# A fused decoder block on one core: the last three passes in an order of their own, and the mixing stage over a ring of seven single-stream PSUM banks

## What is computed

```python
x = x + attention(layernorm(x))          # 32 heads, 8 key/value heads, rope, causal
x = x + autocorrelation(layernorm(x), ctx, ctx)   # 8 heads; FFT correlation, top 9 lags, softmax, shifted sum
x = x + ffn(layernorm(x))
```

```python
H_res  = sinkhorn_log(x_norm @ W_res.T + base)    # 4x4, 50 iterations: rows, then columns normalised
H_pre, H_post = softmax(...), softmax(...)        # 4 each
H_res  = (1 - g) * I + g * H_res
y      = (sum_n x_streams[n] * H_pre[n]) @ W_branch
out[i] = sum_j H_res[i, j] * x_streams[j] + y * H_post[i]
```

## Time and profile before

| | |
|---|---|
| runs | 1224.99 us median of 3 (1220.55 to 1226.48) |
| profiled execution, its own time | 1223.23 us |
| its span, first to last instruction | 1221.4 us |
| mean granted TensorE clock | 0.931 of full speed |
| PE, DVE, ACT, POOL busy | 84%, 75%, 49%, 36% of the span |

### The profile page before, as it was taken

One profiled execution on the slowest core, in us unless ns is written; L12 is line 12 of the kernel. 1 busy time (PEld: TensorE's weight loads), 2 busy tenths in 40 slices (PEclk: granted clock), 3 DMA queues, 4 the chain that ended last, 5 costly groups with the idle time before them and its releaser, 6 DMA issues. The chain is left out here.

```text
span 1221.4 us, 23230 instructions
## 1 busy us (share of the span) xinstructions
PE 1028.0 (84%) x7866; PEld 759.1 (62%) x7866; DVE 921.5 (75%) x2819; ACT 596.9 (49%) x1789; POOL 442.5 (36%) x619
## 2 busy tenths in 40 slices
PE   5889999999999999999657999999999897615056
PEld 4667777777777787777445677776555554313034
DVE  6756787666787666786614878778999999996994
ACT  6534545544555544455515667766564564212023
POOL 0613443333443333443313766663433343110020
PEclk9989999999999999999778999999999998857579
DMA  9011011111011111011132222422222211148025
GB/s 380 29 59 42 17 58 58 58 58 41 22 53 58 58 58 41 29 48 42 45 102 86 87 91 74 130 91 74 89 92 97 77 54 39 44 135 326 0 52 138
DMA packets 47234, 95.71 MB, mean 78 GB/s; under 512 B 5952, under 2 KB 30400, under 8 KB 47168
## 3 DMA queue, kind: packets, MB, share of 16 engines
q1 hardware_dynamic: 47168, 94.91, 23.1%
HBM read 64.48 MB, written 27.26 MB: 75 GB/s over the span
## 5 line engine op out<-in xcount | busy, mean ns | idle before, releaser
L628 POOL TENSOR_TENSOR prob_G<-prob_G,rl 128x512 f32<-128x512 f32 x96 | 99.8, 1041 | 250.4 <-DVE rl L513 250.4
L390 ACT ACTIVATE prob_G<-prob_G,negm 128x128 f32<-128x128 f32 x384 | 148.8, 388 | 83.9 <-DVE negm L455 83.9
L245 PE MATMUL ps_qkv<-w_hi,xT_hi 128*128 128x512 f32 x384 | 156.3, 407 | 17.4 <-DVE prob_G L518 9.2
L246 PE MATMUL ps_qkv<-w_lo,xT_hi 128*128 128x512 f32 x384 | 151.0, 393 | 0.0
L247 PE MATMUL ps_qkv<-w_hi,xT_lo 128*128 128x512 f32 x384 | 150.8, 393 | 0.0
L319 PE MATMUL ps_qkv<-wo_hi,aT_hi 128*128 128x512 f32 x256 | 108.5, 424 | 0.0
L321 PE MATMUL ps_qkv<-wo_hi,aT_lo 128*128 128x512 f32 x256 | 102.6, 401 | 0.0
L320 PE MATMUL ps_qkv<-wo_lo,aT_hi 128*128 128x512 f32 x256 | 102.4, 400 | 0.0
L245 PEld LDWEIGHTS ps_qkv<-w_hi,xT_hi 128*128 128x128 f32 x384 | 72.7, 189 | 44.6 <-issue 21.8
L451 DVE TENSOR_TENSOR prob_G<-ps_s,mask 128x512 f32<-128x512 f32 x96 | 64.9, 676 | 44.4 <-PE ps_s L228 43.9
L480 DVE TENSOR_TENSOR xT_lo<-ps_t,xT_hi 128x512 fp32r<-128x512 f32 x16 | 11.1, 692 | 100.2 <-ACT xT_hi L418 100.2
(11 more groups left out here) (252 smaller groups left out, 2658.2 us busy)
## 6 DMA issues: line engine op xcount, KB each, us to landing
xin<-in_x SPq DMA_DIRECT2D x16, 512.0 KB, 3.3
xres<-in_x SPq DMA_DIRECT2D x16, 512.0 KB, 5.5
x<-xres SPq DMA_DIRECT2D x16, 512.0 KB, 2.6
c_xin<-x SPq DMA_DIRECT2D x16, 512.0 KB, 4.3
c_b_xres<-x SPq DMA_DIRECT2D x16, 512.0 KB, 3.2
rows_x<-c_row SPq DMA_DIRECT2D x64, 128.0 KB, 2.3
m_xm<-rows_x SPq DMA_DIRECT2D x16, 512.0 KB, 8.7
out<-m_ot SPq DMA_DIRECT2D x64, 128.0 KB, 2.4
```

Source lines behind the costliest of these rows:

```text
L245: nc.tensor.matmul(ps_qkv[:, n, :], xT_hi[:, k, :], w_hi[:, k, cols], start=k == 0, stop=False)
L246: nc.tensor.matmul(ps_qkv[:, n, :], xT_hi[:, k, :], w_lo[:, k, cols], start=False, stop=False)
L390: r = nc.scalar.activation(prob(g)[:, j, :], prob(g)[:, j, :], ACT.Exp, bias=negm[:, h:h + 1], accum_out=lsum[:, h:h + 1])
L628: nc.gpsimd.tensor_tensor(prob(g), prob(g), rl[:, g * GROUP:(g + 1) * GROUP].rearrange("p (j o) -> p j o", o=1).to_broadcast([P, GROUP, T] ...
```

## The change

- Chain a gets steps earlier: 10 instead of 6 by the end of pass 6, and 40 instead of 2 in pass 7; its halfway logarithms fall in pass 10 instead of 11. Chain b gets 14 steps instead of 6 in pass 14, chain a 15 instead of 40.
- In pass 14 the weights of row 15 are scaled on DVE, in eight instructions of 128x128, instead of one of 128x1024 on POOL (L1436).
- Passes 15 to 17 are replaced by a function `ending` on PE, ACT and DVE. The products of row 15 are done in halves of 512 columns; no logarithm stands before the copies of the transposed weights on ACT; the DVE takes 2 steps of each of two chains before it waits for the first spectrum (before: `steps_to` of passes 15, parts 0 and 1, up to a's step 306 and b's 22), and counted steps of chain b stand between its other instructions (`fill`). Chain c is begun in full (8 steps) before the two last `branch_in`. At its end chain b is at step 108 and chain c at 50.
- The mixing phase: `p_out` becomes a ring of seven banks, each with one stream of one row; the branch product (`branch_part`) is issued before the row product (`row_part`) of the same row. The branch's diagonals (`post_diag`) are made for all 16 rows at the start, in eight POOL instructions of 256 elements; the row's diagonals in four instructions of 128 elements (DVE: two of 256). The means are spread once, at the start. PE selects chain c's coefficients between the branch and the row product of row 11. ACT takes chain b's halfway logarithms before the copies of chain a, and does no output in between.

```diff
@@ steps_to, logs_at
+        def begun_in(b, chain):
+            for part, to in ((0, 2), (1, 3), (5, 6), (2, 7), (3, 8)):
+                steps_to[b, part] = ((chain, to),)
+            for k, part in enumerate((5, 6, 1, 7, 2)):
+                logs_at[b, part] = ((chain, k + 1),)
+        begun_in(6, one_a)
+        steps_to[6, 4] = ((one_a, 10),)
+        at = 10
+        for b in range(7, B - 2):
...
+        begun_in(B - 2, one_b)
+        steps_to[B - 2, 2] += ((one_a, END[2]),)
+        steps_to[B - 2, 4] = ((one_b, 14),)
+        logs_at[B - 2, 2] += ((one_a, 9), (one_a, 10))
@@ DVE, pass 14
+                    if isinstance(b, int) and c == LAST:
+                        for i in range(KD):
+                            nc.vector.tensor_scalar(wgt[:, i, :], wgt[:, i, :], wrec[:, i:i + 1], None, ALU.mult).then_inc(w_done, 1)
@@ DVE, ending (n = 15)
+                advance(dve, one_a, END[3])
+                fill(2)
+                dve.wait_ge(ws_ps, 2 * n + 1)
+                for h in range(2):
+                    product(tw_re, f_b, v_re, h)
+                    product(tw_im, f_b, v_im, h)
+                    fill(1)
+                dve.wait_ge(ws_ps, 2 * n + 2)
+                for h in range(2):
+                    product(tw_re2, f_c, v_im, h)
+                    product(tw_im2, f_c, v_re, h, -1.0)
+                    fill(1)
+                residual(0)
+                fill(6)
+                residual(1)
+                fill(18)
+                gate_logits(n - 1)
+                gate_max(n - 1)
+                fill(14)
+                gate_logits(n)
+                weave(dve, (one_c, FIRST), (one_b, one_b.issued + FIRST))
+                branch_in(n - 1)
+                gate_max(n)
+                both(12)
+                branch_in(n)
+                both(22)
@@ ACT, ending
+                    act.wait_ge(wT_ps, n + h + 1)
+                    nc.scalar.activation(wT[:, h * HALF:(h + 1) * HALF], p_d[:, h, :], ACT.Copy).then_inc(wT_done, 1)
+                normalised_row(n - 1)
+                branch_copy(n - 2)
+                branch_out(n - 2)
+                log(one_a, FIRST_LOGS + 2 * BLOCK_LOGS, FIRST_LOGS + 2 * BLOCK_LOGS)
+                row_turned(n - 1)
...
+                normalised_row(n)
+                row_turned(n)
+                shares(n - 1)
+                log(one_c, 1, FIRST_LOGS)
+                branch_copy(n - 1)
+                branch_out(n - 1)
+                shares(n)
@@ mixing, PE
+            def branch_part(n):
+                pe.wait_ge(post_done, n // 2 + 1)
+                for g in range(NS):
+                    bank_free(NS * n + g - BANKS)
+                    nc.tensor.matmul(stream_out(n, g), post_diag[...], ym[n][lanes, :], start=True, stop=False)
+            def row_part(n):
+                for g in range(NS):
+                    pe.wait_ge(diag_done, NS * n + g + 1)
+                    nc.tensor.matmul(stream_out(n, g), d[...], xm[n][:, g, :], start=False, stop=True).then_inc(mix_ps, 1)
+                elif n == LAST - 2:
+                    branch_part(n)
+                    select(one_c)
@@ mixing, ACT
+            logs(one_b, FIRST_LOGS + 1, FIRST_LOGS + BLOCK_LOGS)
             copies(one_a)
-            take_out(0, 2)
-            logs(one_b, FIRST_LOGS + 1, FIRST_LOGS + BLOCK_LOGS)
-            take_out(2, one_a.n)
+            take_out(0, one_a.n)
             logs(one_c, FIRST_LOGS + 1, FIRST_LOGS + BLOCK_LOGS)
             logs(one_b, FIRST_LOGS + BLOCK_LOGS + 1, FIRST_LOGS + 2 * BLOCK_LOGS)
             copies(one_b)
-            take_out(one_b.first_row, LAST - 1)
+            take_out(one_b.first_row, LAST - 4)
             logs(one_c, FIRST_LOGS + BLOCK_LOGS + 1, FIRST_LOGS + 2 * BLOCK_LOGS)
-            take_out(LAST - 1, LAST)
+            take_out(LAST - 4, LAST - 2)
             copies(one_c)
-            take_out(LAST, B)
+            take_out(LAST - 2, B)
@@ mixing, POOL
+            for first, to in post_parts:
+                nc.gpsimd.tensor_tensor(post_diag[...], fold, post, ALU.mult).then_inc(post_done, 1)
+                    for g in range(NS):
+                        folded, own = by_token(n, g, 1)
+                        nc.gpsimd.tensor_tensor(diag[n % RING][:, g * NS:(g + 1) * NS, :], folded, own, ALU.mult).then_inc(diag_done, 1)
```

More of the change, by code:

```diff
@@ L927, in iterations @@
             body(B - 2, 0, near=True, far=True, last=True, tail=True, ahead=False)
+            if ending is not None:
+                ending()
+                return
             body(B - 1, 1, near=False, far=True, last=True, tail=True, ahead=False)
@@ L1027, in out_half @@
                 def out_half(n):
[L1028 to L1035, removed]
                     for i, part in enumerate((tw_re, tw_im)):
@@ L1137, in _ @@
             pe.wait_ge(fwd_in, 16)
[L1138 removed]
+            iterations(pe, body, ending)
         @block.scalar
@@ L1259, in _ @@
+            iterations(act, body, ending)
         @block.vector
@@ L1387, in _ @@
+            iterations(dve, body, ending)
         @block.gpsimd
@@ L1433, in body @@
                     split_normalised(b + 2)
-                if near:
+                if near and not (isinstance(b, int) and c == LAST):
                     pool.wait_ge(wrec_done, c + 1)
@@ L1498, in mixing_phase @@
         stored = [sem(f"stored{i}") for i in range(2)]
-        COEFS, COPIES = 4, NS + 1
+        COEFS, COPIES = 2, NS
+        post_parts = tuple((n, n + 2) for n in range(0, B, 2))
         block = ctx.enter_context(nc.Block())
@@ L1548, in _, with select @@
         def _(pe):
-            pe.wait_ge(const_in, 32)
-            for chain in chains:
+            def select(chain):
                 rows = slice(chain.first_row, chain.first_row + chain.n)
                 pe.wait_ge(coef_step, COEFS * (group(chain) + 1))
-                if chain is not one_a:
+                if chain is one_a:
+                    pe.wait_ge(mean_done, 1)
+                else:
                     spread_ready(pe, chains[group(chain) - 1])
                 for g in range(NS):
-                    r = nc.tensor.matmul(p_sel[:, g, 0:chain.n * OWN], sel_sb[:, g, :],
+                    r = nc.tensor.matmul(p_sel[:, g, 0:chain.n * N2], sel_sb[:, g, :],
@@ L1557, in _, with bank_free @@
                                          coef[:, rows, :].rearrange("p b k -> p (b k)"), start=True, stop=True)
                 r.then_inc(sel_ps, 1)
-                pe.wait_ge(rows_in[group(chain)], 32 * chain.n)
-                for n in range(chain.first_row, chain.first_row + chain.n):
+            def bank_free(unit):
+                n, g = divmod(unit, NS)
+                if 0 <= unit < NS * LAST:
+                    pe.wait_ge(out_done, unit + 1)
+                elif unit >= 0 and g < 2:
+                    pe.wait_ge(out_done, NS * LAST + 2 * (n - LAST) + g + 1)
+                elif unit >= 0:
+                    pe.wait_ge(out_by_dve, 2 * (n - LAST) + g - 1)
@@ new lines, in _ @@
+            pe.wait_ge(const_in, 32)
+            pe.wait_ge(own_step, 2)
+            for g in range(NS):
+                r = nc.tensor.matmul(p_sel[:, g, 0:B], sel_sb[:, g, :], own_mean[:, :], start=True, stop=True)
+            r.then_inc(mean_ps, 1)
+            select(one_a)
+            for n in range(B):
+                if n == one_b.first_row:
+                    branch_part(n)
+                    select(one_b)
+                elif n == LAST - 2:
+                    branch_part(n)
+                    select(one_c)
+                else:
+                    branch_part(n)
+                row_part(n)
@@ L1662, in _ @@
             left = BASES[1] - 2 - one_c.issued
-            weave(dve, (one_b, one_b.issued + left), (one_c, BASES[1] - 2))
+            both(left)
             advance(dve, one_b, one_b.issued + 3)
@@ L1667, in _ @@
             left = BASES[2] - 2 - one_b.issued
-            weave(dve, (one_b, BASES[2] - 2), (one_c, one_c.issued + left))
+            both(left)
             advance(dve, one_c, one_c.issued + 3)
```

322 lines of the change are left out of this document (230 added, 92 removed).

## The result

| | median, us | runs | ratio to before, 95% |
|---|---|---|---|
| before | 1224.12 | 4 | |
| after | 1202.3 | 4 (1201.11 to 1205.85) | 0.9825 [0.9805, 0.9846] |

The kernel is 21.8 us (1.7%) faster. I had forecast 1211 and a range of 1204 to 1220, so the direction was right, and the measured time lies 1.7 us under the range: the gain, 13 us by the forecast, was too small by 9. The profiled execution took 1201.8 us, its span is 1200.0; the sum that I had made for the span was 1208.7. All times here are of executions in one state, but for one of the four of `v1_warm_ring`, which took 1395.6 us at a mean clock of 0.727 and is left out of that run's time.

The account below looks back on a forecast made before the run. Bound: DVE, as full as PE from pass 8; row 15's logits, DVE's steps and what follows chain c set the end. Span 1221.4 + 1.6 - 12.9 + 9.4 + 0 - 10.8 = 1208.7; forecast 1211 us, range 1204 to 1220.

Parts of the forecast that it names:

- Step 1: Passes 6 to 14: pass 7 +3.3, pass 6 +0.3, pass 14 -2; sum +1.6 us, pass 14 ending at 1026.7.
- Step 2: From pass 14's end to row 15's logits: 33.2 us instead of 46.1, a change of -12.9.
- Step 3: From row 15's logits to the phase's end: 25.8 us instead of 16.4, +9.4.
- Step 4: From the mixing's start to chain b's coefficients: 81.2 us as before, with no idle but more contention.
- contention 5.5 (2 to 10): Mixing, to chain b's coefficients: POOL's some 13 us of work costs DVE 5.5 us (2 to 10), before 2.9.
- Step 5: From chain b's coefficients to the span's end: 41.8 us instead of 52.6, rows 2.6 us apart.
- A: Rival, mixing rows: POOL paces, quarters cost 0.73 and rows stay at 3.3 us; 1219 us, chance 0.12.
- C: Rival, mixing: DVE's idle returns, 3 to 9 us, as ACT is kept too long; 1217 us, chance 0.08.
- D: Rival, whole ring: clock stays at half, a row takes 4.65 us instead of 2.6; 1229 us, chance 0.05.
- B: Rival, ending: row 15's output products at half clock, +4, branch products behind them +2; 1217 us, chance 0.12.
- E: Better case, passes and mixing: contention at its lower bound and pass 7 nearly free; 1204 us, chance 0.07.
- The halfway logarithms' placing: Mixing: ACT takes chain b's halfway logarithms with nothing queued in front, so DVE's 9.1 us of idle goes.

Follow-up runs that it names:

- v1_warm_ring: Kernel after, plus twenty matmuls without use ahead of chain b's select and four behind it; 1200.4 us (median of three), ratio 0.9811.
- x1: Mixing phase of the kernel after behind the passes of the kernel before; 1216.8 us, ratio 0.9933.
- x7: x1 with ACT taking chain c's last logarithms after the copying-out of rows 9 and 10 instead of between rows 8 and 9; 1213.6 us, ratio 0.9909.
- m1: Kernel after, plus 75 POOL instructions of 128 elements without use, behind row 4's diagonals; ran once, 1208.0 us.

## Why the prediction was off

- **What bounds the kernel**, and that each edit acts through DVE's steps, row 15's logits and the rows' pace, held. So did c's select, which waited for row 10 and not for c (c's coefficients 1178.6, select 1182.09).
- **What I read in the earlier trace rows.** "Busy for all but 9.1 us" was too strong: the first and the last window leave 1.7 and 4.3 us more of idle, most of it in gaps under 0.12 us between dependent steps.
- **Step 1** (passes, +1.6): passes 6 to 14 cost 1.0 in this profile: pass 7 4.2 instead of 3.3, pass 14 -1.0 instead of -2, pass 10 -1.0, and pass 8 -1.7, which I had at nothing. That last one is luck: in six of nine profiles with the same passes, pass 8 is 1.4 to 1.5 longer. That pass 14 still ended 0.7 late comes from ahead of pass 6, where nothing is changed and this execution was 1.35 behind.
- **Step 2** (33.2 to the logits): 32.8. Inside it I had the output products at 4 x 1.02 for each half; their records overlap, a half took 3.5, which made up for a spectrum and last logits at the half clock (3.41 and 3.61; 1.96 and 1.97 with fillers).
- **Step 3** (25.8 to the phase's end) failed by 3.3 us, on size. I charged 3.1 for each `branch_in` and its four pairs and 1.5 for waits on ACT's exponentials. They took 2.6 and 2.3, and no wait was there: woven steps fill them. The eight first pairs took 4.0, not 4.8. Without the longer pause of this execution the step would have been off by 4.2.
- **Step 4** (81.2 to b's coefficients) failed by 3.9, all of it in the term "contention 5.5 (2 to 10)", the largest miss of the sum. POOL ran for 12.5 us beside the weave, about the 13 I wrote, but took 1.6 us. I had taken twice the 2.9 us of before for twice the POOL time. A short instruction can hold only a two-input step, and only for what is left of it: 0.08 us each, by the run with 75 of them. Part of the miss is chance: x1 and x7 show 4.0 for the same POOL work, inside my bounds.
- **Step 5** (41.8) was 1.9 too long: to c's select 21.95 instead of 22.1, from there to the last product 13.2 instead of 14.5 (select to row 0.6 less, and the last rows at 2.57 and with the branch product no longer at the end), and 4.75 instead of 5.2 behind it. The ring's worth was right, as the run with four banks shows.
- **Rivals.** A (POOL paces), C (idle returns) and D (ring at half clock) didn't happen: rows are 2.57 us apart at clock 0.99, and four quarters take POOL 1.5 us. The Trainium skill (TensorE: Matmul & The Clock Gate, "A second HAM failure mode: psum-queue depth-cycling"), named in the prediction beside the clock, has short idles between groups let the clock fall and rise. Idles of 0.7 us a row did not do that before, and the ring has almost none (PE busy for 26.35 of 26.40 us), so it is not seen here and hardly tested. B didn't happen for the output products (1.02 each), but the spectrum and the last logits did run at half clock, inside my sum for step 2. Nearest came E, by half of its reasons: the contention was even under its lower bound of 2, but pass 7 cost 4.2 us and was not nearly free, and steps 3 and 5, which E does not name, gave 5.2.
- **The halfway logarithms' placing.** I credited it with the 9.1 us of idle. The sum came out right, the reason was wrong: with the old order on ACT 0.9 us of idle returns, and b's coefficients come 1.3 us later.
- **The chances** for "faster" add up to 0.89, not 0.88.

So what failed is the sizes of terms: contention in step 4 (5.5 against 1.6), `branch_in` and the waits in step 3, and the pace and ends in step 5, all to the same side and by 9.1 us together. The range took its low end from E alone (1204) and had no case for that.

## What to carry to other kernels

Price two engines' contention per instruction and by what the other engine's instruction reads, not by busy time: beside these steps of 0.2 to 0.35 us, POOL pieces of 0.39 us cost a fifth of their length, those of 1.04 us half, and a handful of them can be far off that mean. Where two halves of a change meet in one engine's queue, the gain of each alone says little; look which wait stands ahead of which in that queue when the timing shifts. And an engine that was idle ahead of a serial tail is worth keeping busy with matmuls that nobody needs, if they end before the real work is ready.

## What was unexpected of the hardware

- The same passes, 7 to 14, take 208.1 us in one execution and up to 212.6 in others. The pass behind a gap of 1.9 to 2.0 us on PE runs its first product at clock 1.00 or, in other executions, partly at the half clock, for 1.4 to 1.5 us more (pass 8, 25.72 or 27.1 to 27.3; pass 12, behind the halfway logarithms, 25.43 or 26.80). That explains up to 2.9 us of a spread; pass 14 took 1.5 us more in one profile, and what lies ahead of the passes, where nothing is changed, spreads by 3.8 us by itself. What decides the clock stays open: in m1 it fell ahead of the gap, and with the gap taken out of pass 7 it fell behind the one in pass 9.
- The step of DVE held by POOL is stretched to 1.16 us by a 1.04 us instruction and to 0.54 by a 0.39 us one; steps with one input are not.
